# Layer 1 attention: keys and queries turned by vector-engine blocks and a trip through memory instead of TensorE, projections two slots further ahead, a second bank for output tiles

## The reference

```python
q = (x @ Wq + bq).reshape(b, n, 32, 128)
k = (x @ Wk + bk).reshape(b, n, 32, 128)
v = (x @ Wv + bv).reshape(b, n, 32, 128)
q = rmsnorm(q, gq); k = rmsnorm(k, gk)              # over the 128 of a head
scores = einsum('bhnd,bhmd->bhnm', q, k) / sqrt(128)
out = einsum('bhnm,bmhd->bnhd', softmax(scores), v)
y = out.reshape(b, n, 4096) @ Wo + bo
x = layernorm(x + y)
```

## Time and profile before

| | us |
|---|---|
| median of 3 runs | 3015.43 (3014.38 to 3015.74) |
| profiled execution | 3014.27 |
| its span | 3012.2 |
| TensorE's mean granted clock | 0.988 |

### The profile page before, as it was taken

The page is one execution under the profiler, slowest core; times in us unless marked ns, Lnnn a source line. Parts: engine busy times, 40 slices in busy tenths (PEclk is TensorE's granted clock), DMA queues, the critical chain, the costliest instruction groups (busy, mean ns, idle before and its releaser), DMA issues. The chain is left out here.

```text
span 3012.2 us, 55470 instructions
## 1 busy us (share of the span) xinstructions
PE 2886.1 (96%) x15712; PEld 2507.4 (83%) x15712; DVE 2233.1 (74%) x3421; ACT 1590.3 (53%) x3145; POOL 1954.0 (65%) x1524
## 2 busy tenths in 40 slices
PE   6999999999999977999999999999999999986998
PEld 5888888888888757889898989998898989975886
DVE  6787887887887756677777777777777777775555
ACT  4444444444444423666666666666666666652221
POOL 7777777777777632666666566666666666655664
PEclk9999999999999989999999999999999999998999
DMA  4334334334334301666666656565666666565551
GB/s 124 115 107 122 101 107 121 101 109 120 100 111 122 119 25 51 192 202 201 202 199 199 208 193 205 192 207 195 206 204 194 204 194 205 194 198 181 151 143 42
DMA packets 310073, 464.10 MB, mean 154 GB/s; under 512 B 30464, under 2 KB 220928, under 8 KB 305792
## 3 DMA queue, kind: packets, MB, share of 16 engines
q1 hardware_dynamic: 272336, 328.37, 37.8%
q10 hardware_dynamic: 37680, 135.02, 11.3%
HBM read 293.41 MB, written 169.87 MB: 154 GB/s over the span
## 5 line engine op out<-in xcount | busy, mean ns | idle before, releaser
L1603 ACT ACTIVATE b_prob<-b_s_ps,b_shift 128x1024 f32<-128x1024 f32 x256 | 286.1, 1117 | 348.2 <-DVE b_shift L1753 341.0
L82 PE MATMUL b_pj_kq<-b_w_hi,xT_hi 128*128 128x384 f32 x1008 | 351.9, 349 | 25.3 <-DVE b_nat L1729 23.9
L83 PE MATMUL b_pj_kq<-b_w_lo,xT_hi 128*128 128x384 f32 x1008 | 342.8, 340 | 0.0
L84 PE MATMUL b_pj_kq<-b_w_hi,xT_lo 128*128 128x384 f32 x1008 | 342.7, 340 | 0.0
L1759 DVE STREAM_TRANSPOSE b_blocks<-b_prob 128x1024 f32<-128x1024 f32 x256 | 317.3, 1240 | 27.3 <-ACT b_prob L1603 26.7
L1510 POOL TENSOR_TENSOR b_rstd<-b_mean_sq,power 128x4 f32<-128x4 f32 x128 | 129.0, 1008 | 319.8 <-DVE b_mean_sq L1739 313.4
L1525 POOL TENSOR_TENSOR b_pT_lo<-b_pT_lo,b_pT_hi 128x1024 fp32r<-128x1024 f32 x128 | 305.1, 2406 | 18.0 <-ACT b_pT_hi L1592 17.6
L1525 POOL TENSOR_TENSOR pT_lo<-pT_lo,pT_hi 128x1024 fp32r<-128x1024 f32 x128 | 305.1, 2407 | 13.1 <-ACT pT_hi L1592 13.1
L1753 DVE TENSOR_REDUCE b_shift<-b_s_ps 128x1 f32<-128x1024 f32 x256 | 306.9, 1199 | 2.7 <-PE b_s_ps L84 2.7
L82 PEld LDWEIGHTS b_pj_kq<-b_w_hi,xT_hi 128*128 128x128 f32 x1008 | 190.4, 189 | 62.0 <-DVE b_nat L1729 47.6
L1284 POOL TENSOR_TENSOR b_w_lo<-b_w_raw,b_w_hi 128x512 fp32r<-128x512 f32 x96 | 124.2, 1295 | 151.4 <-ACT b_w_hi L1277 133.7
(11 more groups left out here) (333 smaller groups left out, 9372.9 us busy)
## 6 DMA issues: line engine op xcount, KB each, us to landing
bounce<-b_blocks ACTq DMA_DIRECT2D x256, 512.0 KB, 3.5
pT_lo<-bounce SPq DMA_DIRECT2D x512, 128.0 KB, 3.1
b_pT_lo<-bounce SPq DMA_DIRECT2D x512, 128.0 KB, 2.8
kv_bounce<-a_kv_blocks SPq DMA_DIRECT2D x128, 256.0 KB, 4.1
a_kv_raw<-kv_bounce SPq DMA_DIRECT2D x32, 1024.0 KB, 4.8
b_w_raw<-in_w SPq DMA_DIRECT2D x32, 768.0 KB, 5.1
b_w_raw<-in_w SPq DMA_DIRECT2D x95, 256.0 KB, 3.2
a_w_raw<-in_w SPq DMA_DIRECT2D x32, 256.0 KB, 3.1
```

What stands on the lines that cost most here:

```text
L82: pe.matmul(out, w_hi, x_hi, start=first, stop=False, skip_group_check=partial)
L83: pe.matmul(out, w_hi, x_lo, start=False, stop=False, skip_group_check=partial)
L84: return pe.matmul(out, w_lo, x_hi, start=False, stop=last, skip_group_check=partial)
L1603: act.activation(prob[t % 2][:, :], s_ps[t % 2][:, :], ACT.Exp, bias=shift[:, t:t + 1], accum_out=row_sum[:, t:t + 1]).then_inc(exp_done, 1)
```

## The change

- `transpose_kq` on PE is gone. In its place DVE turns 32x32 blocks of the scaled keys and queries of a batch (`turn_kq`, two instructions, first in the odd slot), ACT writes them to memory (`write_kq`, one DMA of 256 KB, behind `write_blocks`), SP reads them back (`move_kq`, four DMAs of 64 KB in rows of 512 bytes), and `kq_high` and `kq_low` read the result from SBUF. `kq_low` takes three instructions instead of two.
- Projections run four tiles ahead instead of two (`projected`), and `square`, `means`, the inverse root and `scale_kq` one batch further ahead (`prepared`), with a second buffer for `nat` of batch 0. `kq_high` and `kq_low` stay in the slots where they were.
- In the odd slot `kq_high` is now first on ACT, and `kq_low` comes ahead of `transpose_blocks` on DVE.
- SP: `move_kq` of a batch stands behind `move` of an even tile; the loads of weights and bias stand ahead of `move` of tile 4.
- The bank half that the transposes used is the bank of odd output tiles (`y_odd`); an output tile waits for the addition of the tile two before, not one before.
- The casts of weights are in slots 0, 1 and 2 instead of 1, 2 and 4; casts of values are in slots 1, 5 (two) and 7 instead of 1, 3, 5 and 7; some semaphores are merged.

The diff, cut to its core:

```diff
-            return pj if peeled(h, HEADS - 1) and t >= 3 and t % 2 else y_ps[:, :]
+            return y_odd if t % 2 else y_ps[:, :]
...
-            if s < 6:
-                return (h + 1, 1 - b, s + 2) if nxt else None
-            return (h + 2, b, s - 6) if more else None
+            if s < 4:
+                return (h + 1, 1 - b, s + 4) if nxt else None
+            return (h + 2, b, s - 4) if more else None
+
+        def prepared(h, b, nxt, more, s):
+
+            i = s // 2 + 1
+            if i < NB:
+                return (h + 1, 1 - b, i) if nxt else None
+            return (h + 2, b, 0) if more else None
...
-        SPLITS = {1: 0, 2: 1, 4: 2}
+        def v_batches(h, b, cur, nxt, s):
+
+            if s == 1:
+                return ((h, b, 3),) if cur else ()
+            which = {5: (0, 1), 7: (2,)}.get(s, ())
+            return [(h + 1, 1 - b, i) for i in which] if nxt else ()
+
+        SPLITS = {0: 0, 1: 1, 2: 2}
...
+            def move_kq(g, i):
+
+                sp.wait_ge(kq_written, 16 * (NB * g + i + 1))
+                sp.sem_inc(room, 1)
+                wait(sp, kq_lo_done, NB * g + i - 1)
+                for c in range(GROUPS):
+                    sp.dma_start(kq_raw[i % 2][c * BLK:(c + 1) * BLK].rearrange("y r k u x -> y r (k u x)"),
+                                 kq_bounce[i % 2][:, :, c, :].rearrange("r y n -> y r n")).then_inc(kq_moved, 16)
+
             def step(h, b, cur, rest, nxt, more):
+
+
                 if cur and more:
                     aw.load(sp, w, h + 2)
                     load_bias(h + 2, b)
-                if rest:
-                    move(h - 1, NT - 1)
-                for t in range(NT - 1):
+                for t in range(NT // 2, NT):
+                    if rest:
+                        move(h - 1, t)
+                    if t == 4 and cur:
+                        move_kq(h, 3)
+                    if t == 6 and nxt:
+                        move_kq(h + 1, 0)
+                for t in range(NT // 2):
                     if cur:
                         move(h, t)
+                    if t % 2 == 0 and nxt:
+                        move_kq(h + 1, t // 2 + 1)
                     if nxt and t == 2:
...
             def kq_high(g, bg, i):
                 cut = slice(i * WIDE, (i + 1) * WIDE)
-                act.wait_ge(kq_tr, NB * g + i + 1)
+                act.wait_ge(kq_moved, 16 * GROUPS * (NB * g + i + 1))
                 wait(act, scored, NT * (g - 1))
-                act.activation(k_hi[bg][:, cut], kq_ps[:, 0, :], ACT.Copy)
-                act.activation(q_hi[bg][:, cut], kq_ps[:, 1, :], ACT.Copy, scale=gain[:, 0:1]).then_inc(kq_hi_done, 1)
+                act.activation(in_blocks(k_hi[bg][:, cut]), from_blocks(i, 0), ACT.Copy)
+                act.activation(in_blocks(q_hi[bg][:, cut]), from_blocks(i, 1), ACT.Copy,
+                               scale=gain[:, 0:1]).then_inc(kq_hi_done, 1)
+
+            def write_kq(g, i):
+
+                act.wait_ge(kq_blocked, 2 * (NB * g + i + 1))
+                wait(act, kq_written, 16 * (NB * g + i))
+                wait(act, kq_moved, 16 * GROUPS * (NB * g + i - 1))
+                act.dma_start(kq_bounce[i % 2][:, :, :, :].rearrange("r y c n -> (r y) (c n)"),
+                              kq_blocks[i % 2][:, :, :, :, :].rearrange("p c k u x -> p (c k u x)")).then_inc(
+                    kq_written, 16)
...
-                        v_high(*v_batch(h, b, cur, nxt, s))
+                    ready = prepared(h, b, nxt, more, s)
+                    if nxt and s % 2:
+                        kq_high(h + 1, 1 - b, s // 2)
+                    if s % 2 == 0 and ready:
...
-                    if nxt and s % 2 == 0:
-                        scale_kq(h + 1, 1 - b, s // 2)
+                    if s % 2 == 0 and ready:
+                        scale_kq(*ready)
                     if rest and s == 0:
                         write_blocks(h - 1, NT - 1)
                     if cur and s:
                         write_blocks(h, s - 1)
-                    if nxt and s % 2:
-                        kq_high(h + 1, 1 - b, s // 2)
+                    if s % 2 and ready:
+                        write_kq(ready[0], ready[2])
                     if cur:
...
-            def transpose_kq(g, i):
-                pe.wait_ge(kq_scaled, NB * g + i + 1)
-                wait(pe, kq_lo_done, NB * g + i)
-                for kind in range(2):
-                    for u in range(BATCH):
-                        last = pe.transpose(kq_ps[:, kind, u * P:(u + 1) * P], nat[i][:, u, kind * HD:(kind + 1) * HD],
-                                            sh.ident[:, :])
-                last.then_inc(kq_tr, 1)
...
-                wait(pe, y_added, NT * h + (t - 1 if peeled(h, HEADS - 1) and t >= 3 else t))
+                wait(pe, y_added, NT * h + t - 1)
...
             def kq_low(g, bg, i):
                 cut = slice(i * WIDE, (i + 1) * WIDE)
                 dve.wait_ge(kq_hi_done, NB * g + i + 1)
-                dve.tensor_tensor(k_lo[bg][:, cut], kq_ps[:, 0, :], f(k_hi[bg][:, cut]), ALU.subtract)
-                dve.scalar_tensor_tensor(out=q_lo[bg][:, cut], in0=kq_ps[:, 1, :], scalar=gain[:, 0:1],
-                                         in1=f(q_hi[bg][:, cut]), op0=ALU.mult,
-                                         op1=ALU.subtract).then_inc(kq_lo_done, 1)
+                dve.tensor_tensor(in_blocks(k_lo[bg][:, cut]), from_blocks(i, 0), f(in_blocks(k_hi[bg][:, cut])),
+                                  ALU.subtract)
+                for u in range(BATCH):
+                    one = slice(i * WIDE + u * P, i * WIDE + (u + 1) * P)
+                    last = dve.scalar_tensor_tensor(
+                        out=q_lo[bg][:, one].rearrange("p (r x) -> p r x", r=GROUPS), in0=kq_raw[i % 2][:, :, 1, u, :],
+                        scalar=gain[:, 0:1], in1=f(q_hi[bg][:, one]).rearrange("p (r x) -> p r x", r=GROUPS),
+                        op0=ALU.mult, op1=ALU.subtract)
+                last.then_inc(kq_lo_done, 1)
+
+            def turn_kq(g, bg, i):
+
+                dve.wait_ge(kq_scaled, NB * g + i + 1)
+                wait(dve, kq_written, 16 * (NB * g + i - 1))
+                for k in range(2):
+                    dve.transpose(kq_blocks[i % 2][:, :, k, :, :].rearrange("p c u x -> p u c x"),
+                                  nat_of(bg, i)[:, :, k * HD:(k + 1) * HD].rearrange(
+                                      "p u (c y) -> p u c y", c=GROUPS)).then_inc(kq_blocked, 1)
...
-                    if nxt and s % 2 == 0:
-                        means(h + 1, s // 2)
+                    ready = prepared(h, b, nxt, more, s)
+                    if s % 2 == 0 and ready:
+                        means(ready[0], ready[2])
+                    if s % 2 and ready:
+                        turn_kq(*ready)
                     if projected(h, b, nxt, more, s):
                         take(*projected(h, b, nxt, more, s))
+                    if nxt and s % 2:
+                        kq_low(h + 1, 1 - b, s // 2)
...
                     if q and q[3]:
@@ -1806,8 +1866,6 @@
                         transpose_blocks(h - 1, NT - 1)
                     if cur and s:
                         transpose_blocks(h, s - 1)
-                    if nxt and s % 2:
-                        kq_low(h + 1, 1 - b, s // 2)
                     for t in scored_in(h, cur, s):
```

85 lines of the change are left out of this document (44 added, 41 removed).

## The result

The changed kernel takes **3337.47 us** (median of 4 runs, 3334.53 to 3341.9), against 3014.9 for the kernel before (4 runs beside it, 3012.31 to 3015.74): a ratio of 1.107, 95% interval 1.1056 to 1.1084. The profiled execution took 3341.9 us, its span is 3340.0.

What follows compares the result with a forecast made beforehand. A DVE and ACT ring was taken as the bound, PE a fraction behind. Four pairs at 13.5 plus 1.2 for weights give 55.2 us a head, +7.2; 31 heads 223, head 0's trip 8: +231, 3246 us, range 3110 to 3370.

Steps and rivals of the forecast that it cites:

- the ring: DVE, ACT and SP orders closing a loop through memory, kq_low to next odd slot's kq_low: 13.5 us a pair; chance 0.74.
- the prediction's own sign of being wrong: Wrong if kq_high on ACT starts right behind an exponent, or if heads repeat in under 48 us.
- Link 4: From the write's issue on ACT to SP's first issue of that tile's move: 3.91 us, bounds 2.9 to 6.7.
- link 5: On SP, the four issues of the even tile's move standing ahead of move_kq: 2.02 us.
- link 6: From move_kq's first issue on SP to kq_high on ACT: 4.5 us, bounds 3.8 to 5.8.
- the rival of the short trip: Memory landings near their least, 12.2 to 12.4 us a pair, +1.3 us a head, some 3060 us; chance 0.13.
- Link 1: kq_low on DVE, three instructions instead of two: 0.83 us, against 0.73 before.
- the rival on the other side: Memory trip hidden, shorter DVE chain decides: 11.23 us under PE's 11.45, about 46.4 us a head, 2965 us; chance 0.04.
- The casts in other slots: Short pieces on ACT, said to move between places that have slack once the ring decides; no cost priced.
- The weights' load at +1.2 a head: 768 KB load issued shortly ahead of tile 4's write delays it once a head: 1.2 us, bounds 0 and 1.9.
- The clock: TensorE's clock falls in pauses; a quarter more gives 14.3 us a pair, 3330 us; chance 0.09 together with contention.
- The +45 us estimated from the Trainium skill's fit: Transfers at 2.0 us plus bytes at 436 GB/s: links 4 and 6 at 3.5 and 3.6, ring 12.2, whole +45 us.

Runs made afterwards that it cites:

- the eighth kernel: Changed kernel with loads and kq moves reordered, kq_low behind transposition, SP writing kq, GpSimd waiting, weight casts ahead of exponents in slots 1, 3: 3083.15 us, ratio 1.0226.
- the three orders together: Changed kernel with weights' load behind tile 4's moves, move_kq ahead of the even tile's move, kq_low behind the transposition of probabilities: 3148.65 us, ratio 1.0453.

## Why the prediction was right or wrong

Slower, and within the range: 3246 was forecast, 3337 measured, an increase of 323 us for 231. But that the size came out near is in good part luck: the term that carried the forecast, the ring at 13.5 us in every pair, held in none of the ordinary pairs, and the prediction's own sign of being wrong came true in three pairs of four, nearly every time: `k_hi` starts right behind an exponent or the cast that follows it (2051.10, 2038.25).

- *The ring sets every pair at 13.5 us:* wrong in three pairs of four. Link 4 was 2.65, not 3.91; link 5, 1.93 for 2.02; link 6, 2046.91 to 2051.10, 4.19 for 4.5 with `k_hi` not waiting, and 3.7 by the landing estimated above. With these the ring is some 12.4 us (2.00 + 1.25 + 2.65 + 1.93 + 3.7 + 0.84) and just hidden. These links were the rival of the short trip, which I gave 0.13; why the trip is that short, with the DMA engines about as busy in the two heads (0.61 against 0.63), isn't shown.
- *Link 1, `kq_low` at 0.83:* it took 1.93 us in that pair and 2.62 in pair 2. I took the durations of the old instructions, bounded by up to 0.15 for the third, and overlooked that their operands move from PSUM to SBUF.
- *What took the ring's place:* the chain of DVE and ACT, which I had priced as 0.44 us shorter than before under the rival on the other side. That shortening is real: of the 5.72 us from exponent to exponent, 0.53 is the cast and 1.10 the excess of the low parts over 0.83; without them 4.09 would stand, against 4.69. It was eaten by the two things that I had put at nothing, the casts and the growth of the low parts beyond 0.1.
- *The casts in other slots, between places that have slack:* no slack. Behind an even exponent a cast cost nothing before, since ACT stood idle for 1.0 us behind it (ahead of `k_hi` at 2029.30); now `k_hi` stands there, and the casts of slots 0 and 2 (2037.72) hold it up by 0.53 us each, in pairs 1 and 2. The two casts ahead of a square were on the chain before and still are.
- *The weights' load at +1.2 a head:* pair 4 grew by 6.0, of which the run with both loads moved took back 3.4 to 3.6. I took it from one row in which the write stood 1.71 us behind the load; here it stands 0.41 us behind, and the landing of the load itself went from 5.1 to 7.1 us in the median. The upper bound of 1.9 was no bound.
- *Loop start:* 3.2 us for each two heads, 1.6 a head, not foreseen. The rows of ACT's order could not have shown it; the queue of instructions does, afterwards.
- *The clock:* 0.94 in the window above, with pauses of PE of up to 5.8 us. As forecast, it isn't what decides: PE's work fits into the longer pairs. No run takes the clock apart.
- *DVE's turns at 0.4 us each, beside the path:* 0.42 in the median, and hidden behind the projection; right. PE's share of 87%: 88%. *Nearly all of 124 batches wait 2.4 us:* 44 of 109, 29 of them for 2.7 to 6.1 us, about one a head, in pair 4. *Heads repeat every 55 us:* 58.6.
- *The removed transposes' 1.7 us a head are a gain only where nothing else sets the pair:* right, and seen in the eighth kernel, whose pairs 2 and 3 fall to 11.0 and 11.4.
- *The +45 us estimated from the Trainium skill's fit:* a ring of 12.2 gives 4 x 12.2 - 48.0 = 0.8 us a head, or 2.0 with the load's 1.2, so 33 or 70 us with the 8 of head 0; the 45 doesn't follow from it. It lies near the short-trip rival's 1.3 us a head, which give 48.

The Trainium skill's fit ("DMA: Bandwidth & Descriptors", "Anatomy of one DMA", written there for the GpSimd path), 3.2 us for the write and 2.15 for the read, was nearer to the landings here (2.9 and 2.4) than the median of before that I preferred; for the load the same estimate would be 3.8, and it landed in 7.1. And the same Trainium skill's "SBUF — State Buffer", section "SBUF: two separate sides", has the rule that I had missed: a VectorE instruction with two inputs in SBUF and a GpSimd instruction that reads SBUF lock each other out for the whole instruction. By an estimate from that rule 0.60 us should become 0.60 plus the overlap, 1.28 with 0.68 beside it and 2.61 with 2.01; the traces have 1.09 and 2.13. They agree in direction, but the growth is 0.7 to 0.8 of the overlap and not all of it.

## What to carry to other kernels

A trip through memory must be priced with the order of its neighbours: where the low parts, which consume it, stand in VectorE's queue was worth half of this loss when it alone was changed, and the place of the bulk load a quarter; the three orders together gave 189 us and not the sum of 314. When an operand moves from PSUM to SBUF, look up what GpSimd does in that moment. And before work is taken from the fullest engine, look for idle time ahead of instructions that wait anyway: moving four casts into it, two of which had been on the chain, gave 25 us (3014.74 to 2990.01), where no version that took the transposes from PE came under the kernel before. When two kernels are compared pair by pair, anchor the pairs at a row that stands in the same slot in both.

## What was not expected of the hardware

- Two SBUF operands: two `q_lo` last 0.60 us alone, 1.09, 1.66 and 2.13 with 0.68, 1.49 and 2.01 us of GpSimd's work beside them; one operand in PSUM: 473 to 477 ns in all 115 cases, with up to 0.47 us of it.
- Taking one DMA issue a pair, with its waits, out of ACT's loop body took away 64 packets on the queue of instructions and the 4.2 us of waiting at each start of the body; 40 copies a body, added to the kernel before, brought neither.
- A write of 512 KB 0.41 us behind a load of 768 KB was ready for SP after 7.82 us, against 2.65 where no load went out just ahead. The kernel with the load in three parts and one cast moved took 3114 us, against 3083 with the load whole.
